# Expert numbers of eight tiles packed in one integer and unpacked in each engine's registers

## The reference, cut to what matters

```python
logits = jnp.einsum('bsh,he->bse', jax.lax.stop_gradient(x), W_g)
probs = jax.nn.softmax(logits, axis=-1)
top_w, top_idx = jax.lax.top_k(probs, K)                 # K = 2 of E = 8
h = jnp.einsum('bsh,ehf->bsef', x, w1) + b1              # 128 -> 512
h = jax.nn.gelu(h, approximate=False)
expert_out = jnp.einsum('bsef,efh->bseh', h, w2) + b2    # 512 -> 128
sel = jnp.take_along_axis(expert_out, top_idx[..., None], axis=2)
out = jnp.einsum('bskh,bsk->bsh', sel, top_w)
```

## Time and profile before

| | us |
|---|---|
| median of 3 runs (lowest, highest) | 414.41 (410.16, 415.88) |
| the profiled execution's own time | 414.85 |
| its span in the profile | 413.1 |
| PE busy | 324.6 (79%) |
| DVE busy | 243.4 (59%) |
| ACT busy | 221.4 (54%) |
| POOL busy | 168.9 (41%) |

### The profile page before, as it was taken

One profiled execution on the slowest core, in us unless ns is written; L12 is line 12 of the kernel. 1 busy time (PEld: TensorE's weight loads), 2 busy tenths in 40 slices (PEclk: granted clock), 3 DMA queues, 4 the chain that ended last, 5 costly groups with the idle time before them and its releaser, 6 DMA issues.

```text
span 413.1 us, 7019 instructions
## 1 busy us (share of the span) xinstructions
PE 324.6 (79%) x2119; PEld 269.8 (65%) x2119; DVE 243.4 (59%) x635; ACT 221.4 (54%) x399; POOL 168.9 (41%) x172
## 2 busy tenths in 40 slices
PE   4998899899898988404658677778689499999990
PEld 1443886767794654204647576668689399999990
DVE  4797736579211679796225445444457278888870
ACT  2699849669456783302524444544456055565650
POOL 2366262900000157100745556655554134554541
PEclk9999999999998999955579989887899799999996
DMA  7998000000009300005211211121121523333210
GB/s 230 330 361 272 2 0 2 1 3 0 2 2 299 108 0 1 0 1 217 54 53 58 63 55 60 49 62 53 60 59 63 131 70 102 107 99 99 68 33 6
DMA packets 20997, 33.39 MB, mean 81 GB/s; under 512 B 5070, under 2 KB 14963, under 8 KB 20322
## 3 DMA queue, kind: packets, MB, share of 16 engines
q1 hardware_dynamic: 16194, 23.86, 18.5%
q0 software_dynamic: 4256, 9.08, 7.3%
q10 hardware_dynamic: 512, 0.00, 0.1%
HBM read 19.14 MB, written 14.99 MB: 83 GB/s over the span
## 4 chain that ended last, share of the span: by engine, by line
PE 49%; DVE 15%; issue 7%; ACT 6%; another core or an unknown queue 5%; DMA 2%; DVEq 0%; POOLq 0%; POOL 0%; ACTq 0%; SPq 0%
PE bank L686 15%; PE bank L695 15%; DVE Z L1003 4%; PE bank L502 3%; PE bank L679 3%; PE bank L617 2%; PE bank L597 2%; PE bank L596 2%; DVE p2T L1195 2%; ACT p2T L859 2%; PE bank L624 1%; PE bank L667 1%; PE bank L635 1%; PE bank L607 1%
## 5 line engine op out<-in xcount | busy, mean ns | idle before, releaser
L686 PE MATMUL bank<-xgT,p2T 128*128 128x128 f32 x608 | 91.6, 299 | 20.3 <-DVE xgT L1189 19.9
L859 ACT ACTIVATE p2T<-p2T 128x512 f32<-128x512 f32 x76 | 47.9, 630 | 100.7 <-DVE p2T L1195 74.9
L686 PEld LDWEIGHTS bank<-xgT,p2T 128*128 128x128 f32 x608 | 82.8, 211 | 23.3 <-DVE xgT L1189 22.2
L695 PE MATMUL bank<-Z,p2T 128*128 x608 | 87.2, 289 | 9.2 <-ACT p2T L859 9.0
L695 PEld LDWEIGHTS bank<-Z,p2T 128*128 128x128 f32 x608 | 78.7, 202 | 12.3 <-issue 12.1
L1195 DVE TENSOR_TENSOR p2T<-bank,b1T 128x512 f32<-128x512 f32 x76 | 52.5, 691 | 25.2 <-PE bank L686 17.6
L431 POOL DMA_INDIRECT out<-ZA x38 | 37.4, 983 | 46.8 <-DVE ZA L1210 25.3
L426 POOL DMA_INDIRECT brows<-ZA x38 | 38.2, 1006 | 40.6 <-DVE ZA L1210 33.5
L1205 DVE TENSOR_TENSOR yb<-bank,b2s 128x128 f32<-128x128 f32 x76 | 22.1, 290 | 51.7 <-PE bank L695 28.3
L418 POOL DMA_INDIRECT ZA<-xrows,idx x38 | 37.3, 982 | 32.7 <-DVE idx L1181 21.4
L865 ACT ACTIVATE p2T<-Z 128x512 f32 x76 | 46.6, 614 | 0.0
(11 more groups left out here) (207 smaller groups left out, 495.9 us busy)
## 6 DMA issues: line engine op xcount, KB each, us to landing
brows<-blank SPq DMA_DIRECT2D x1, 5016.0 KB
ZA<-brows SPq DMA_DIRECT2D x38, 132.0 KB
Z<-in_z SPq DMA_DIRECT2D x4, 1024.0 KB, 8.0
xrows<-XR SPq DMA_DIRECT2D x1, 2176.0 KB, 7.2
Z<-in_w SPq DMA_DIRECT2D x1, 2048.0 KB, 9.4
ZA<-xrows,idx POOLq DMA_INDIRECT x38
brows<-ZA POOLq DMA_INDIRECT x38
out<-ZA POOLq DMA_INDIRECT x38
```

What stands on the lines that cost most here:

```text
L686: mm = pe.matmul(bank[2 + n % 2][:, k * P:(k + 1) * P], w1t[:, n % 2, k * P:(k + 1) * P], xgT[:, n % 2, :], start=True, stop=True)
L695: mm = pe.matmul(bank[6 + n % 2][:, 0:P], hg[:, n % 2, k * P:(k + 1) * P], w2s[:, bass.ds(e * F + k * P, P)], start=(k == 0), stop=(k == K ...
L859: act.activation(hg[:, n % 2, :], hs[:, n % 2, :], ACT.Gelu).then_inc(s["fge"], 1)
```

## The change

DVE multiplies each tile's number by 8 to the power of its place among eight neighbours (`power8`, filled by eight POOL memsets near the start), sums eight by eight, and leaves ten integers in `tile_w` (`WORDS` = 10). The table's computation goes from one step after the count to three. PE, ACT and DVE each load one value for eight tiles, so 10 loads an engine in place of 19, of one value in place of four. `value_load` also brings a check of the value's bounds, two register instructions behind each load, which the old call had left out. Each use then has a shift and a mask.

```diff
+WORDS = -(-TILES // 8)
...
-        def load_experts(eng, expert_of, quad):
-
-            _, vals = nc.values_load_multi_w_load_instructions(
-                tile_e[0:1, 4 * quad:4 * quad + 4], engines=(eng.engine,), min_val=0, max_val=E_ - 1,
-                skip_runtime_bounds_check_because="the table's entries are a count of 0 to 8, cut at 7")
-            expert_of[quad] = vals
+        def load_experts(eng, expert_of, w):
+
+            expert_of[w] = eng.value_load(tile_w[0:1, w:w + 1], min_val=0, max_val=8 ** 8 - 1)
+
+        def expert(expert_of, t):
+
+            return (expert_of[t // 8] >> (3 * (t % 8))) & 7
...
-                    for quad in range(TILES // 4):
-                        if quad not in expert_of and 4 * quad <= t + 3 < 4 * quad + 4:
-                            load_experts(eng, expert_of, quad)
+                    w = (t + 3) // 8
+                    if w not in expert_of and 0 <= t + 3 < TILES:
+                        load_experts(eng, expert_of, w)
...
+            for k in range(8):
+                pool.memset(power8[:, k:k + 1], float(8 ** k)).then_inc(s["cst"], 1)
...
             def down(n):
-                e = expert_of[n // 4][n % 4]
+                e = expert(expert_of, n)
...
             def w1_copy(n):
 
-                e = expert_of[n // 4][n % 4]
+                e = expert(expert_of, n)
...
+            dve.memset(tef[:], 0.0).then_inc(s["te_set"], 1)
...
-            dve.tensor_reduce(tef[:], te, AX.X, ALU.add).then_inc(s["te_set"], 1)
             dve.wait_ge(s["te_set"], 3)
-            dve.tensor_scalar(tile_e[:], tef[:], float(E_ - 1), None, ALU.min).then_inc(s["te_set"], 1)
+            dve.tensor_reduce(tef[:].rearrange("p w k -> p (w k)")[:, 0:TILES], te, AX.X, ALU.add).then_inc(s["te_set"], 1)
+            dve.wait_ge(s["te_set"], 4)
+            dve.scalar_tensor_tensor(tef[:], tef[:], float(E_ - 1), power8[:].unsqueeze(1).to_broadcast([P, WORDS, 8]),
+                                     ALU.min, ALU.mult).then_inc(s["te_set"], 1)
+            dve.wait_ge(s["te_set"], 5)
+            dve.tensor_reduce(word[:], tef[:], AX.X, ALU.add).then_inc(s["te_set"], 1)
+            dve.wait_ge(s["te_set"], 6)
+            dve.tensor_copy(tile_w[:], word[:]).then_inc(s["te_set"], 1)
...
             def add_b1(n):
-                e = expert_of[n // 4][n % 4]
+                e = expert(expert_of, n)
```

## The result

| | before | after |
|---|---|---|
| median of 4 runs each (lowest, highest), us | 414.56 (410.16, 415.88) | 424.29 (421.99, 427.42) |
| the profiled execution's own time | 414.85 | 421.99 |
| its span in the profile | 413.1 | 420.1 |

A forecast was written before the change was run, and what follows sets the result against it. POOL sets the pace until 302 us, then PE's work (3.80 us per two tiles) tied with a loop through DVE and ACT (3.81). Terms +6.6 + 0 + 0 + 0.3 = +6.9 us, 421.3 us against the median; range 414 to 427.

The forecast's parts named there:

- Shift and mask on the loop: Behind PE's and DVE's waits in the later tiles: each step shows in full on the two-tile loop, +6.6 us.
- One sign: In the profile after, from 331 us on: PE idle about 0.15 us a tile ahead of `down`, put down to `gelu`.
- The size of a step: One shift or mask on PE or DVE: 0.08 us, between 0.05 and 0.11, so +4.1 to +9.1 us in all.
- ACT: Shift and mask ahead of `w1_copy` are worked off while `gelu` runs: 0; uncovered, 0.2 us a tile.
- Fewer loads: In the later tiles, the old loads' visible cost and that of new loads with checks cancel: 0, ends -0.7 and +0.8.
- The POOL-paced regime: Some 25 tiles, 8.5 rounds: POOL's work and way back unchanged, 0; ends +3.7 and -1.4 us.
- Filling the loop, table and constants: First tile of each half passes the chain uncovered, +0.3 us; extra table steps and memsets hide in idle time, 0.
- the steps are hidden: Rival: PE's and DVE's shift and mask run under running work, about 414 us; chance 0.15.
- the loads count in full: Rival: PE's 19 removed loads save their full 0.37 us each, net -5.1 us, 409.3 us; chance 0.05.
- faster by over 2%: Outcome for the whole kernel: a time below 406 us; chance 0.04.
- The dearer steps: Rival: each step at the two waits costs 0.14 us, +11.8 us, 426.2 us; chance 0.25.
- the forecast itself: The main case for the whole kernel: 418.5 to 424 us; chance 0.55.

The follow-up runs named there:

- e10: The kernel before, old loads of four, with shift and mask on all three engines only in tiles 28 to 75; 421.34 us against 415.68, ratio 1.017.
- e3: The changed kernel with shift and mask written as explicit register instructions one tile ahead, before the waits, check kept; 419.86 us against 415.12 of before, ratio 1.011.
- e8: The changed kernel with shift and mask ahead of the waits and without the bounds check; 418.72 us against 415.72 of before, ratio 1.006.
- e5: The kernel before, old loads, plus shift and mask on PE alone; 420.91 us, ratio 1.013 (the next run, on DVE alone: 419.62 us, 1.010).
- e7: The kernel before, old loads, plus shift and mask on ACT alone; 415.48 us against 415.72, ratio 1.000.
- e1: The kernel before with its old table layout and loads of four, plus only a shift and a mask at each use; 424.72 us against 415.12, ratio 1.021.
- e2: The changed kernel without the bounds check behind each load; 424.38 us against 415.12 of before, ratio 1.021.
- e9: The kernel before, old loads of four, with shift and mask on all three engines only in tiles 0 to 27; 417.04 us against 415.68, ratio 1.005.
- e11: The kernel before with loads of eight values in place of four, no packing and no register steps; 416.21 us against 415.68, ratio 1.000.
- e12: The kernel before with its loads of four, no check, plus shift and mask ahead of the waits; 421.88 us against 416.83, ratio 1.010.

## Why the prediction was right, and where it was not

**Shift and mask on the loop: right.** They were forecast at +6.6 us for 44 tiles behind the waits for `fm1` and `fge`, as two tied lengths, 3.80 and 3.81 us, of which one grows. The loop measures 4.15 us, a tile 2.08 us (forecast 2.07), the gap between `gelu` and `down` 0.34 against 0.14 us, that between `up` and `add_b1` 0.30 against 0.14 (forecast 0.16 more; measured 0.16). One sign was put wrongly: I wrote that PE would stand idle ahead of `down`, put down to `gelu`. In this stretch the profile puts 1.2 us in two places down to it, and the rest of the wait hides under the last pass of `up`; DVE's 7.2 us and the count of matmuls show it instead. The 44 tiles are borne out for the 37 of the second part alone. The other seven stand behind the rounds in the first half, and there e10's trace is 1.1 us longer than that of before, which its earlier tile 30 hides. e3 and e8 show that it is the place behind the wait, e5 to e7 that only PE's and DVE's steps lie on the loop and that they add up.

**The size of a step: slightly low.** I took 0.08 us between 0.05 and 0.11, the middle of two bounds; that it came so near is in part luck. PE's is 0.092 and DVE's 0.076, mean 0.084; the whole term by that is 82 x 0.084 = 6.9 us. In the trace of after the second part, with 37 of the 44 tiles and so 18.5 x 3.74 = 69 of the 82 steps, grew by 6.3 us, 0.091 each with the check in it. The term was short by 0.3 to 0.9 us.

**ACT: right.** 0 forecast, e7 measures 1.000 (0.996 to 1.003).

**Fewer loads: right in the sum.** 0 forecast, with ends of -0.7 and +0.8. The second parts bear it out: 71.4 us in e8, with the loads of after and no check, against 71.2 before, and 77.5 in both after and e1. The check's first instruction takes 0.15 us on PE and 0.19 on DVE, above the 0.11 that I had as its bound, and costs 0.4 us between after and e2. The Trainium skill ("Runtime: NRT & Kernel Launch", section Instruction fetch mechanics) gives some 200 ns for each register of a TENSOR_LOAD. The loads from SBUF here show no such price: on PE one value takes 0.31 us, four 0.33 to 0.38 and eight 0.67.

**The POOL-paced regime: the step that failed.** I wrote that POOL's work does not change, that its way back is `add_b2`, which got no steps, and took 0, with +3.7 as the upper end. e9 measures +2.1 us (0.7 to 3.5) for steps in tiles 0 to 27 alone. The length of a full round was right (10.2 us forecast; 287.37 to 297.56 after, 10.17 in e9). These two rows of after show it beside the earlier trace rows:

```profile
287.37 1.00 POOL L432 DMA_INDIRECT brows<-ZA  x1 [2.72 <-DVE ZA L1223]
...
297.56 1.00 POOL L432 DMA_INDIRECT brows<-ZA  x1 [2.69 <-DVE ZA L1223]
```

The number of rounds was not right, and I had named a change of it as a sign of being wrong. From tile 5 to tile 26 DVE let POOL's scatter wait at eight tiles before (5, 8, 11 and so on to 26) and at nine after (5, 7, 10, 12, 15, 18, 20, 23 and 26). What I left out is that a stretch is more than its round: it has a start and an end, and some rounds before were shorter than the one that I read (9.54 us from 257.90 to 267.44, with an idle time of 1.91). In the profiled executions the first part is 133.5 to 133.8 us in the four kernels that have none there on PE or DVE (before, e7, e10, e11) and 135.3 to 139.8 in the ten with steps on PE or DVE there. It is so whether they stand behind the waits or ahead of them (e3, e8, e12), so it is not the closed loop. TensorE's granted clock, which is lower in this stretch (0.87 before from 212 to 302 us, 0.80 after), does not sort the kernels either: e8 and e9, which lost, have 0.89, and e10 and e11, which lost nothing, 0.84 and 0.83. I did not find the mechanism. That the rounds stand one tile earlier in e9 and e8, and for the most part in e1 and e12, is seen in single executions. But in e3, which lost 1.5 us, they start at the same tiles as before up to tile 20, and in e7 and e11, which lost nothing, they move as well. So it is not the whole of it, and it stays open whether the steps set it.

**Filling the loop, table and constants: not disproved, too small to be told.** For filling, four steps on each of two chains at 0.08 us make 0.6 us and not the 0.3 that I put into the sum. The table's cover shrank and held. DVE after, beside the 1.23 us of the earlier trace rows:

```profile
191.58 0.20 DVE L1189 TENSOR_SCALAR vt<-bank 128x38 f32<-128x38 f32 x1 [0.70 <-PE bank L673]
```

DVE still waits 0.70 us for the rank matmuls.

**The rivals.** That the steps are hidden (414) is out: all runs of after lie above 421, and the loop is longer. That the loads count in full (409) is out by e8. Its own 409.3 is also within 2% of before, so the 0.04 that I gave to faster by over 2% had nothing behind it. The dearer steps (426.2 at 0.14 us each) came near in the time, but not in their reason: a step was 0.08 to 0.09, and 2.1 us of the difference came from the first regime. The measured 424.29 lies nearer to their 426.2 than to my 421.3; it is above the 418.5 to 424 of the forecast itself and inside the wide range of 414 to 427 only because that takes in most of the dearer case. By size: forecast 6.9 = 6.6 + 0.3; measured 7.2 (e10) + 2.1 (e9).

None of the versions beats the kernel before. The loads of eight tie with it.

## What to carry to other kernels

A register instruction between a semaphore wait and the work that it releases was paid in full here, 0.08 to 0.09 us each, as the wait lies on a closed loop as long as the busiest engine's own work; so follow one loop of the data and compare its length with the engine's before you call anything hidden. Put the arithmetic ahead of the wait with explicit register instructions and read in the stream where the builder has placed it, but mind the sequencer's lead, which the loads use up too. And the loads that packing removes were hidden already, but for 0.06 us of each 0.37, so there was next to nothing to save: price what a change removes from a row, before what it adds.

## What the runs showed of the hardware

- A single register operation has a record of 36 ns on PE, 45 on DVE and 38 on ACT, shorter than the 46 and 57 of an offset step on PE and DVE, and costs 0.092 us on PE and 0.076 on DVE on the loop. PE's is the shorter record and the dearer step, by single traces in which each cost can be off by 0.01.
- A load into registers takes on PE 0.31 us for one value, 0.33 to 0.38 for four and 0.67 for eight: nearly flat to four, then not. I had expected about 0.4 for eight.
- The check of a loaded value is a fused step of 151 ns on PE and 190 on DVE, over three times an offset step, and an assertion of 18 ns (23 on DVE).
- Where the steps stand ahead of the waits, one load with its check sets PE's sequencer back by 0.27 us of idle time and some 0.5 us of the chain; one without the check costs 0.18.
- In the stretch that POOL paces, two steps of under 0.1 us a tile on PE or DVE lengthened the first part by 1.5 to 6 us in single executions, and by 2.1 us (0.7 to 3.5) in the timing of e9, while full rounds kept their length. Why is open.
- A wait of one engine for another can leave no idle time in the records: a loop longer by 0.34 us in two tiles took 9% of the matmuls out of a stretch and 2% of PE's busy time.
